# Engine loops over four tiles in two sorted expert mixtures, and who copies the weights

## The chip, the cores and the metric

The program runs on one core of a Trainium2 chip. The metric is the device time of one execution in microseconds. The core's engines are PE (TensorE: matrix products and transposes), DVE (VectorE), ACT (ScalarE), POOL (GpSimd) and SP (SyncE, which here only issues transfers). Each has its own instruction stream; they meet at semaphores.

## The reference, cut to what matters

A network of four layers on 128 graphs of 40 nodes with 128 features, 5120 tokens in all; each layer is a graph step and an expert mixture or another token step. Two of the mixtures are computed by sorted tiles in the kernel, layer 1's and layer 3's:

```python
def _L1_ffn_ref(x, gamma, beta, Wr, br, W1, b1, W2, b2):   # E = 8 experts, top 2, 128 -> 256 -> 128
    xn = (x - mu) * rsqrt(var + EPS) * gamma + beta
    logits = einsum('bsd,de->bse', xn, Wr) + br
    top_vals, top_idx = top_k(logits, 2)
    w = softmax(top_vals); w_full = ...                      # the gate of each token for each expert
    for e in range(E):
        h = gelu(einsum('bsd,dh->bsh', xn, W1[e]) + b1[e])
        y = y + (einsum('bsh,hd->bsd', h, W2[e]) + b2[e]) * w_full[..., e, None]

def _L3_ffn_ref(x, Wg, bg, W1, b1, W2, b2):                 # the same with 8 experts, top 2, gates of 1
    ...
```

Layer 2's token step is a graph attention over 524288 edges (plus one loop a node) that yields gate scores. For it the kernel must know, for each node, how many edges with a source beyond the tokens point at it. That count is independent of the mixture of layer 1, and the kernel does it beside that mixture:

```python
src = concatenate([edge_index[0], loops]); dst = concatenate([edge_index[1], loops])
e = leaky_relu(a_src[src] + a_dst[dst], 0.2)
ee = exp(e - segment_max(e, dst)[dst]); denom = segment_sum(ee, dst)
```

## The kernel before

`graph_network` calls the layers in order; each stage has one instruction stream for every engine, and a stage ends when all its engines are done. In the two sorted mixtures a router picks two experts for each token and gives each of the 10240 pairs of token and expert a place in a list that is sorted by expert and padded to tiles of 256 rows. `ex.NT` = 47 tiles is the most that this can need, and all 47 are always computed. `ex.table` holds the expert of each tile, `ex.gidx` the token of each place, `ex.pidx` the two places of each token.

`sparse_moe` is run twice: for layer 1 with `count` (an `EdgeCount`) and for layer 3 without it. A tile i goes through these steps.

- POOL gathers its 256 token rows from DRAM by two indirect transfers of 128 rows (L1126), into one of `NX` = 6 buffers. It may write tile i once PE has transposed tile i-6 (semaphore `x_ps`).
- PE transposes the rows (`turned`, L1148).
- ACT moves the transposed rows out of PSUM (`moved`, L1192, or L1194 with layer 1's scale and shift), and copies the expert's 642 columns of weights into one of `NW` = 3 buffers (`fetch`, L1209).
- PE does the hidden products (`hidden`, L1157), ACT the two gelus (`gelus`, L1202), PE the output products (`outer`, L1165).
- DVE adds the bias and writes the result (`result`, L1229), SP stores it to DRAM (L1281), from one of `NY` = 4 buffers.

The order on each engine is fixed by the Python loops, which write out all 47 tiles. PE's is: transposes of tile i+2, hidden products of i+1, output products of i. ACT's: gelus of i, move of i+2, copy of the weights of i+2.

Behind the tiles, when all stores have landed, POOL gathers the two result rows of every token (L1138): 8 parts of 5 token tiles, ten indirect transfers a part, 80 in all, into 6 buffers. DVE adds each part into the residual (L1268 with gates in layer 1, L1270 in layer 3), and in layer 3 SP stores the output.

The edge count of layer 1 works on `keys`, 4096 numbers in each partition. `find` (L1882) takes the eight largest of a segment, `strike` (L1887) puts zero in their place. Segments of 64 come first (64 of them), then segments of 256 (16); in the kernel before DVE does two finds and two strikes beside each tile, over tiles 0 to 41. Then `rest` (L1912 to L1916) tests how many keys are left and takes the largest number over the partitions, PE turns that column (`count_left`, L1952), and `size` makes from it the number of turns of a wide search. `digits` (L1891 to L1902) splits the 640 keys found into two digits, and then the keys are counted in 40 batches of 16: `one_hot` (L1908, L1909) writes two comparison tables, and `counts` (L1957) multiplies them in PE, 16 products into one accumulator. Two table buffers are used in turn, so DVE's batch c waits for PE's batch c-2 (`h_ps` of the count), and PE's batch c waits for DVE's (`hot`). In the kernel before all 40 batches come behind the tiles, five ahead of each of the eight parts' additions. `finish` (L1932 on) is last: a loop with a number of turns from the data, each with four finds and strikes over 1024 keys, the digits, and two batches; then the sums are copied out (L1944), and the next layer can begin.

```python
for n in range(PARTS):                       # DVE, behind the tiles
    if count is not None:
        step = count.KS // count.HG // PARTS
        for c in range(n * step, (n + 1) * step):
            count.one_hot(dve, c, c % 2, c * count.HG)
```

## Time and profile before

| what | us |
|---|---|
| median of 3 runs | 3664.99 |
| the runs | 3655.89 to 3667.97 |
| the profiled execution | 3670.82 |
| its span, first to last instruction | 3669.0 |
| DVE, PE, ACT, POOL busy in it | 2320.1, 2788.3, 1256.7, 584.0 |

The profile is of one execution. A row of a timeline gives the start from the beginning of the span, the duration, the engine, the line, the operation, what it writes and reads, and in brackets how long the engine was idle before it and what ended that, as far as the profile can tell. Rows of one line that follow each other closely are merged (x8). PE's ends are modelled, since its products are pipelined. The name of a releaser that is an input transfer of long ago ("DMA xin") stands for one the profile could not tell. PEclk is the granted clock as a share of full speed; DMA is the busy share of the 16 transfer engines.

### The profile page before, as it was taken

The page shows a single profiled execution, that of the slowest core. Times are in us where ns is not written, and L with a number is a line of the kernel's source. Part 1 is how long each engine was busy: PE and PEld are TensorE (multiplying, and loading weights), DVE is VectorE, ACT ScalarE, POOL GpSimd, SP SyncE. Part 2 cuts the span into 40 slices and gives each one's busy share as a digit, 9 for nine tenths or more (in the row PEclk, how much of TensorE's full clock was granted, in tenths as well). Part 3 has the DMA queues.
Part 4 walks back from the last instruction along what each step waited for, and adds up shares of the span by engine and source line. Part 5 has one row for each costly group of instructions (what it writes and reads, how often), then busy time and mean ns, then how long its engine had stood idle before and what let it go on. Part 6 is the DMA issues. An engine that isn't in the chain of part 4 may idle for free. (4 is left out here: it accounts for less than half of the span.)

```text
span 3669.0 us, 53910 instructions
## 1 busy us (share of the span) xinstructions
PE 2788.3 (76%) x20509; PEld 1774.0 (48%) x20509; DVE 2320.1 (63%) x4225; ACT 1256.7 (34%) x2409; POOL 584.0 (16%) x561
## 2 busy tenths in 40 slices
PE   6479999999999999463575249699876989985660
PEld 5234555555555555252264237366543666652550
DVE  6736777777777777468535395788993346765111
ACT  3333434444344444143262004222112444543440
POOL 0000000000000000100165400133220013420556
PEclk7689999999999999766597556799987987886785
DMA  3312111121111112112033110000001211102232
GB/s 40 99 39 51 41 39 39 45 56 39 41 52 39 39 39 50 60 35 58 14 87 61 33 16 1 5 0 0 1 0 47 66 41 46 44 16 58 70 80 72
DMA packets 163983, 151.93 MB, mean 41 GB/s; under 512 B 73412, under 2 KB 139344, under 8 KB 161320
## 3 DMA queue, kind: packets, MB, share of 16 engines
q1 hardware_dynamic: 152624, 126.06, 14.0%
q0 software_dynamic: 11136, 22.83, 3.0%
q8 instruction: 148, 2.42, 0.3%
q14 instruction: 75, 0.61, 0.1%
HBM read 123.16 MB, written 25.67 MB: 41 GB/s over the span
## 5 line engine op out<-in xcount | busy, mean ns | idle before, releaser
L2821 PE MATMUL hy_ps<-hy_uT,hy_win 128*128 128x512 f32 x1152 | 498.7, 594 | 0.0
L2821 PEld LDWEIGHTS hy_ps<-hy_uT,hy_win 128*128 128x128 f32 x1152 | 217.6, 190 | 281.2 <-issue 281.2
L2882 PE MATMUL hy_ps<-hy_wo,hy_yg 128*128 128x512 f32 x512 | 245.0, 624 | 10.1 <-ACT XNP L3018 8.6
L2347 PE MATMUL er_c<-XNG 128*128 128x400 f32 x544 | 205.1, 517 | 24.6 <-POOL XNG L2278 24.4
L1791 POOL IOTA iof<- 128x128 f32 x1 | 0.2, 243 | 1394.6 <-POOLq L2494 1394.6
L1126 POOL DMA_INDIRECT f_xg<-f_xn,f_gidx x188 | 178.2, 948 | 173.8 <-POOLq L893 76.7
L1229 DVE TENSOR_TENSOR f_ysl<-f_py,f_cur 128x256 f32<-128x256 f32 x94 | 38.4, 420 | 229.8 <-PE f_py L1165 124.0
L1957 PE MATMUL f_px<-XNG 128*128 128x40 bf16 x736 | 69.2, 266 | 143.3 <-DVE XNG L1909 98.0
L1138 POOL DMA_INDIRECT XNP<-f_y,f_pidx x160 | 160.3, 1002 | 85.0 <-issue 48.1
L2278 POOL TENSOR_TENSOR XNG<-er_VW,er_MD 128x400 f32<-128x400 f32 x136 | 122.3, 899 | 295.5 <-DVEq L2248 196.9
L2292 ACT ACTIVATE er_OT<-er_t 128x384 bf16<-128x384 f32 x128 | 61.0, 489 | 307.9 <-PE er_t L2317 307.9
L1157 PE MATMUL f_ph<-f_xT,f_cur 128*128 128x256 f32 x376 | 110.9, 422 | 60.4 <-issue 54.4
L2882 PEld LDWEIGHTS hy_ps<-hy_wo,hy_yg 128*128 128x128 f32 x512 | 96.0, 197 | 124.8 <-issue 102.9
L3095 DVE TENSOR_TENSOR_SCAN XNG<-XNG,hy_fx 128x2048 f32<-128x2048 f32 x32 | 141.6, 4425 | 2.3
L2347 PEld LDWEIGHTS er_c<-XNG 128*128 128x128 f32 x544 | 98.6, 193 | 85.2 <-POOL XNG L2278 27.8
L2327 PE MATMUL er_g<-er_TP,er_OT 128*128 128x320 bf16 x768 | 130.8, 308 | 10.1 <-ACT er_OT L2292 6.1
L1957 PEld LDWEIGHTS f_px<-XNG 128*128 128x128 bf16 x736 | 60.7, 152 | 151.8 <-DVE XNG L1909 106.0
L836 DVE TENSOR_TENSOR f_hg<-f_hs,f_gb 128x640 f32<-128x640 f32 x64 | 52.7, 825 | 110.1 <-ACT f_hs L818 110.1
L1165 PEld LDWEIGHTS f_py<-f_cur,f_hT 128*128 128x128 f32 x752 | 106.6, 207 | 20.2 <-issue 13.7
L1165 PE MATMUL f_py<-f_cur,f_hT 128*128 128x128 f32 x752 | 108.2, 291 | 10.6 <-issue 10.2
L2969 ACT ACTIVATE hy_xr<-hy_ps 128x512 f32<-128x512 f32 x80 | 47.5, 593 | 178.3 <-PE hy_ps L2821 178.3
L1562 PE MATMUL g_ps<-g_Z,g_wc 128*128 128x320 f32 x256 | 106.1, 562 | 1.1 <-ACT g_Z L1625 1.1
(652 smaller groups left out, 6310.2 us busy)
## 6 DMA issues: line engine op xcount, KB each, us to landing
XNG<-hy_decays SPq DMA_DIRECT2D x32, 1024.0 KB
hy_rb<-hy_inverse SPq DMA_DIRECT2D x128, 128.0 KB, 3.3
f_y<-f_ysl SPq DMA_DIRECT2D x94, 128.0 KB
f_gb<-gate_rows SPq DMA_DIRECT2D x16, 640.0 KB, 5.2
g_KB<-g_keys SPq DMA_DIRECT2D x32, 320.0 KB
f_xn<-XNG SPq DMA_DIRECT2D x4, 1280.0 KB
hy_xn<-XNP SPq DMA_DIRECT2D x1, 4096.0 KB, 14.1
hy_XC<-hy_xn SPq DMA_DIRECT2D x16, 256.0 KB
```

The source lines that it names most:

```text
L1126: pool.indirect_dma_start(out=xg[:, i % NX, h, :], out_offset=None, in_=ex.xn_dram, in_offset=bass.IndirectOffsetOnAxis(ap=ex.gidx[:, n:n ...
L1138: pool.indirect_dma_start(out=yc[:, n % NC_, t, c, :], out_offset=None, in_=ex.y_dram, in_offset=bass.IndirectOffsetOnAxis(ap=ex.pidx[:, n ...
L1157: pe.matmul(psh[i % 2][k], cur[:, i % NW, k * 128:(k + 1) * 128], xT[:, i % 2, :], start=True, stop=True).then_inc(h_ps, 1)
L1165: mm = pe.matmul(psy[i % 2][:, h, :], hT[:, i % 2, k, h * 128:(h + 1) * 128], cur[:, i % NW, H + k * D:H + (k + 1) * D], start=(k == 0), s ...
L1562: mm = pe.matmul(psy, wc[:, h, :], Z[:, c % 2, h].rearrange("p b n -> p (b n)"), start=(h == 0), stop=(h == HD - 1))
L1957: mm = pe.matmul(self.ph, self.OL[:, b, :, k], self.OH[:, b, :, k], start=False, stop=False, skip_group_check=True)
L2278: pool.tensor_tensor(X[:, u % XBUF], VW[:, 1 - par, u, :, None].broadcast_to([128, V, TJ]), MD[:, 1 - par, u, None, :].broadcast_to([128, ...
L2327: pe.matmul(o[:, 0:NS], OT[:, u % 2, j, :], TP[:, i, j * NS:(j + 1) * NS], start=(i == 0 and j == 0), stop=(i == 2 and j == J - 1))
L2347: mm = pe.matmul(flat(acc[j][:]), OD[:, 1 - par, u, j * 128:(j + 1) * 128], flat(X[:, u % XBUF]), start=False, stop=False, skip_group_chec ...
L2821: mm = pe.matmul(p[:], win[:, t, m * 128:(m + 1) * 128], uT[:, t, :], start=(t == 0), stop=(t == KT - 1))
L2882: mm = pe.matmul(PS[4 + q % 2][:], yg[:, t, q * 128:(q + 1) * 128], wo[:, t, :], start=(t == 0), stop=(t == KT - 1))
L3095: dve.tensor_tensor_scan(L[:, a][:, st], dAb[:, a][:, st], E[:, st], 0.0, ALU.mult, ALU.add)
```

## The change

Both mixtures compute 48 tiles, twelve turns of `BODY` = 4. PE, ACT, SP, and in the last mixture DVE, run the first and the last turn written out and those between as a loop of their own (`Fori`), with waits and addresses from a register. POOL stays written out. All three sorts of buffer become four (from 6, 4 and 3). The hidden products of a tile go to one PSUM bank instead of two, and signal once instead of twice. The count gets two banks of its own.

In the last mixture DVE copies the weights, three tiles ahead of its sums; in the first ACT does, as before.

The count of layer 1 is laid out anew. DVE does three finds and strikes of 64 beside each of the first 22 tiles, two of 256 beside each of the next 8, the test of what is left and the digits at tile 30 and the reduction at tile 31. Beside tiles 32 to 47 it writes one batch of tables each, and PE counts that batch behind the output products of the same tile. The wide search comes right behind the tiles, ahead of the parts; the 24 batches that remain come three ahead of each part's additions.

```diff
+BODY = 4
-        self.NT = (2 * T + E * (SL - 1)) // SL
+        self.NT = -(-((2 * T + E * (SL - 1)) // SL) // BODY) * BODY
...
-    NX, NY, NW = 6, 4, 3
+    NX, NY, NW = BODY, BODY, BODY
+    TURNS = NT // BODY
...
-        psh = [[bank(f"ph{i}{k}") for k in range(K)] for i in range(2)]
+        psh = [bank(f"ph{i}").rearrange("p (k n) -> p k n", k=K) for i in range(2)]
         if count is not None:
-            count.borrow(psx[0], psx[1])
+            count.borrow(bank("pc"), bank("pt"))
+            COUNTING = count.FIRST // BODY
...
         def _(pe):
...
                 for k in range(K):
-                    pe.matmul(psh[i % 2][k], cur[:, i % NW, k * 128:(k + 1) * 128], xT[:, i % 2, :], start=True, stop=True).then_inc(h_ps, 1)
+                    mm = pe.matmul(psh[j % 2][:, k, :], cur[:, j % NW, k * 128:(k + 1) * 128], xT[:, j % 2, :], start=True, stop=True)
+                mm.then_inc(h_ps, 1)
...
+            def tiles(r, final=False, counting=None):
+                for j in range(BODY):
+                    if not (final and j + 2 >= BODY):
+                        turned(r + (j + 2) // BODY, (j + 2) % BODY)
+                    if not (final and j + 1 >= BODY):
+                        hidden(r + (j + 1) // BODY, (j + 1) % BODY)
+                    outer(r, j)
+                    if counting is not None:
+                        count.counts(pe, BODY * counting + j, j % 2)
+            turned(0, 0)
+            turned(0, 1)
+            hidden(0, 0)
+            tiles(0)
+            if count is None:
+                with pe.Fori(1, TURNS - 1) as r:
+                    tiles(r)
+                tiles(TURNS - 1, final=True)
+            else:
                 count.count_start(pe)
+                with pe.Fori(1, COUNTING) as r:
+                    tiles(r)
+                with pe.Fori(0, TURNS - 1 - COUNTING) as r:
+                    tiles(r + COUNTING, counting=r)
+                tiles(TURNS - 1, final=True, counting=TURNS - 1 - COUNTING)
                 count.count_left(pe)
-                for c in range(count.KS // count.HG):
-                    count.counts(pe, c, c % 2)
                 count.count_rest(pe)
...
         def _(act):
...
+            def tiles(r, final=False):
+                for j in range(BODY):
+                    gelus(r, j)
+                    if not (final and j + 2 >= BODY):
+                        moved(r + (j + 2) // BODY, (j + 2) % BODY)
+                        if count is not None:
+                            fetch(r + (j + 2) // BODY, (j + 2) % BODY)
...
         def _(dve):
...
+            def fetch(r, j):
+                i = BODY * r + j
+                e = dve.value_load(ex.table[0:1, bass.ds(i, 1)], min_val=0, max_val=E - 1)
+                if not (isinstance(i, int) and i < NW):
+                    dve.wait_ge(y_out, i - NW + 1)
+                dve.tensor_copy(cur[:, j % NW, :], ex.W[:, bass.ds(e, 1), :].rearrange("p a n -> p (a n)")).then_inc(w_cur, 1)
...
+                with dve.Fori(1, TURNS - 1) as r:
+                    for j in range(BODY):
+                        result(r, j)
+                        fetch(r + (j + 3) // BODY, (j + 3) % BODY)
...
+                for i in range(NT):
+                    result(i // BODY, i % BODY)
+                    count.beside_tile(dve, i)
                 count.size(dve)
+                count.wide(dve)
             for n in range(PARTS):
                 if count is not None:
+                    count.beside_part(dve, n, PARTS)
...
+    FIRST, EARLY = 32, 16
...
+    def beside_tile(self, dve, i):
+        fine, mid = EC // self.FINE, EC // self.MID
+        fine_tiles, mid_tiles = -(-fine // 3), mid // 2
+        f = lambda t: min(3 * t, fine)
+        if 1 <= i <= fine_tiles:
+            dve.drain()
+            self.strike(dve, self.FINE, 0, f(i - 1), f(i))
+        if i < fine_tiles:
+            self.find(dve, self.FINE, 0, f(i), f(i + 1))
+        m = i - fine_tiles
+        if 0 <= m <= mid_tiles:
+            dve.drain()
+            if m > 0:
+                self.strike(dve, self.MID, self.KF, 2 * m - 2, 2 * m)
+            if m < mid_tiles:
+                self.find(dve, self.MID, self.KF, 2 * m, 2 * m + 2)
+        if m == mid_tiles:
+            dve.drain()
+            dve.tensor_scalar(self.left, self.keys, 0.0, None, ALU.is_gt)
+            self.digits(dve, slice(0, self.KS))
+        if i == self.FIRST - 1:
+            dve.tensor_reduce(self.seg[:], self.left.rearrange("p (s c) -> p s c", c=WIDE), AX.X, ALU.add)
+            dve.drain()
+            dve.tensor_reduce(self.cnt[:], self.seg[:], AX.X, ALU.max).then_inc(self.counted, 1)
+        if i >= self.FIRST:
+            c = i - self.FIRST
+            self.one_hot(dve, c, c % 2, c * self.HG)
...
-                self.one_hot(dve, KS // HG + r * (KW // HG) + c, c % 2, KS + c * HG)
-        dve.wait_ge(self.h_ps, n * (KW // HG) + KS // HG + 3)
+                self.one_hot(dve, self.EARLY + r * (KW // HG) + c, c % 2, KS + c * HG)
+    def beside_part(self, dve, n, parts):
+        late = self.KS // self.HG - self.EARLY
+        for c in range(n * late // parts, (n + 1) * late // parts):
+            self.one_hot(dve, self.EARLY + self.turns * (self.KW // self.HG) + c, c % 2, (self.EARLY + c) * self.HG)
+    def close(self, dve):
+        dve.wait_ge(self.h_ps, self.turns * (self.KW // self.HG) + self.KS // self.HG + 3)
         dve.tensor_copy(self.g.cntB[:], self.ph)
...
+        late = KS // HG - self.EARLY
+        with pe.Fori(0, late // 2) as r:
+            for c in range(2):
+                self.counts(pe, self.EARLY + n * (KW // HG) + 2 * r + c, c)
```

## Rows read from the trace of the kernel before

**Rows 1.** the page: the span and the chain that ended last, by engine.
```profile
span 3669.0 us, 53910 instructions
...
PE 3%; POOL 2%; issue 1%; another core or an unknown queue 1%; DMA 0%; ACT 0%; DVE 0%; POOLq 0%; ACTq 0%; DVEq 0%
```

**Rows 2.** windows; busy of PE, PEld, DVE, ACT, POOL; PEclk, DMA share, GB/s.
```profile
1811.00:1930.00 119.00, 78.75 (x472) 68.79 (x472) 36.34 (x219) 67.66 (x137) 76.83 (x81) 0.88 0.30 79
...
1966.00:2081.00 115.00, 19.90 (x209) 17.23 (x209) 37.18 (x60) 0.00 (x0) 81.71 (x80) 0.52 0.19 47
2081.00:2186.00 105.00, 49.67 (x529) 43.65 (x529) 100.07 (x184) 0.00 (x0) 0.00 (x0) 0.50 0.00 1
3403.00:3556.00 153.00, 112.57 (x658) 98.25 (x658) 18.74 (x47) 87.08 (x189) 88.72 (x94) 0.86 0.36 80
```

**Rows 3.** timeline of POOL in the first mixture: start us, us, instruction, idle before.
```profile
1875.80 0.94 POOL L1126 DMA_INDIRECT f_xg<-f_xn,f_gidx  x1 [1.26 <-PE f_px L1148]
...
1881.78 0.94 POOL L1126 DMA_INDIRECT f_xg<-f_xn,f_gidx  x1 [1.28 <-PE f_px L1148]
```

**Rows 4.** timeline of PE, same stretch.
```profile
1871.10 1.10 PE L1157 MATMUL f_ph<-f_xT,f_cur 128*128 128x256 f32 x4 [1.79 <-issue]
1872.04 1.05 PE L1165 MATMUL f_py<-f_cur,f_hT 128*128 128x128 f32 x8
```

**Rows 5.** timeline of DVE, same stretch.
```profile
1875.53 0.42 DVE L1229 TENSOR_TENSOR f_ysl<-f_py,f_cur 128x256 f32<-128x256 f32 x1 [3.54 <-PE f_py L1165]
```

**Rows 6.** timeline of DVE at the end of the last mixture's tiles.
```profile
3550.04 0.42 DVE L1229 TENSOR_TENSOR f_ysl<-f_py,f_cur 128x256 f32<-128x256 f32 x1 [1.55 <-PE f_py L1165]
...
3554.67 0.42 DVE L1229 TENSOR_TENSOR f_ysl<-f_py,f_cur 128x256 f32<-128x256 f32 x1 [0.47 <-PE f_py L1165]
```

**Rows 7.** timeline of all engines behind the first mixture's last tile.
```profile
1965.07 0.42 DVE L1229 TENSOR_TENSOR f_ysl<-f_py,f_cur 128x256 f32<-128x256 f32 x1 [0.47 <-PE f_py L1165]
...
1968.14 0.94 POOL L1138 DMA_INDIRECT XNP<-f_y,f_pidx  x1 [18.64 <-DMA f_y<-f_ysl]
...
2029.30 1.53 PE L1957 MATMUL f_px<-XNG 128*128 128x40 bf16 x16 [7.71 <-DVE XNG L1909]
...
2055.65 1.23 DVE L1908 TENSOR_TENSOR XNG<-XNG,ec_dl 128x2048 bf16<-128x2048 bf16 x1 [26.41 <-DMA xin<-in_x_dram]
...
2056.79 0.48 DVE L1909 TENSOR_TENSOR XNG<-XNG,ec_dh 128x640 bf16<-128x640 bf16 x1
...
2072.99 0.94 POOL L1138 DMA_INDIRECT XNP<-f_y,f_pidx  x1 [0.30 <-issue]
2080.89 1.23 DVE L1908 TENSOR_TENSOR XNG<-XNG,ec_dl 128x2048 bf16<-128x2048 bf16 x1 [23.61 <-DMA xin<-in_x_dram]
...
2083.97 2.87 DVE L1268 SCALAR_TENSOR_TENSOR raw<-XNP,f_gates,raw 128x128 f32<-128x128 f32 x10
```

**Rows 8.** timeline of DVE in the wide search and at the layer's end.
```profile
2140.66 4.60 DVE L1882 MAX8 ec_K<-lend 128x8 f32<-128x1024 f32 x4
...
2155.07 4.60 DVE L1882 MAX8 ec_K<-lend 128x8 f32<-128x1024 f32 x4
...
2185.61 0.20 DVE L1944 COPY cntB<-f_px 128x40 f32<-128x40 f32 x1 [1.64 <-PE f_px L1967]
```

**Rows 9.** DVE groups, 1811 to 2187, by form: busy us, mean ns, idle before.
```profile
L1882 DVE MAX8 ec_K<-lend 128x8 f32<-128x64 f32 x64 | 11.0, 214 | 0.0
...
L1914 DVE TENSOR_REDUCE ec_seg<-XNG 128x4 f32<-128x4096 f32 x1 | 4.4, 4420 | 0.1
L1912 DVE TENSOR_SCALAR XNG<-lend 128x4096 f32<-128x4096 f32 x1 | 2.3, 2294 | 0.1
```

**Rows 10.** window of the stage that loops on registers; columns as in rows 2.
```profile
2820.00:2960.00 140.00, 140.00 (x500) 92.11 (x499) 54.62 (x74) 61.10 (x117) 0.00 (x0) 1.00 0.25 66
```

**Rows 11.** windows of DVE's sums (L1229) alone; columns as in rows 2, DVE alone.
```profile
1811.00:1930.00 119.00, 13.40 (x32) 0.88 0.30 79
```

**Rows 12.** POOL's gathers behind both mixtures (L1138): count, min/median/max ns.
```profile
L1138 POOL DMA_INDIRECT XNP<-f_y,f_pidx x160: 940/944/1679, 1968.1 to 3659.4; - x160
```

More of the change, by code:

```diff
@@ L1127, in gather @@
                                             in_offset=bass.IndirectOffsetOnAxis(ap=ex.gidx[:, n:n + 1], axis=0)).then_inc(x_in[i % NX], 16)
[L1129 to L1130 removed]
             for b in range(NY):
[L1132 removed]
+                pool.wait_ge(y_st[b], 16 * TURNS)
             for n in range(PARTS):
@@ L1203, in gelus @@
                 ins.then_inc(h_out, 1)
-            def fetch(i):
-                e = act.value_load(ex.table[0:1, i:i + 1], min_val=0, max_val=E - 1)
-                if i >= NW:
-                    act.wait_ge(y_out, i - NW + 1)
-                act.activation(cur[:, i % NW, :], ex.W[:, bass.ds(e, 1), :].rearrange("p a n -> p (a n)"), ACT.Copy).then_inc(w_cur, 1)
-            act.wait_ge(ex.w_in, 16 * (2 * K + 2))
-            for i in range(NW):
-                fetch(i)
-            moved(0)
@@ L1215, in _ @@
-            moved(1)
-            for i in range(NT):
-                gelus(i)
-                if i + 2 < NT:
-                    moved(i + 2)
-                if i >= 1 and i - 1 + NW < NT:
-                    fetch(i - 1 + NW)
+            def tiles(r, final=False):
[5 more added lines that the diff above has]
+                            fetch(r + (j + 2) // BODY, (j + 2) % BODY)
@@ L1223, in _ @@
+            act.wait_ge(ex.w_in, 16 * (2 * K + 2))
+            if count is not None:
+                fetch(0, 0)
+                fetch(0, 1)
+            moved(0, 0)
+            moved(0, 1)
+            tiles(0)
+            with act.Fori(1, TURNS - 1) as r:
+                tiles(r)
+            tiles(TURNS - 1, final=True)
         @block.vector
         def _(dve):
-            def result(i):
-                dve.wait_ge(y_ps, i + 1)
-                if i >= NY:
-                    dve.wait_ge(y_st[i % NY], 16 * (i // NY))
-                dve.tensor_tensor(y[:, i % NY], psy[i % 2], cur[:, i % NW, None, 2 * H:2 * H + D].broadcast_to([128, SLH, D]), ALU.add).then_inc(y_out, 1)
@@ new lines, in _ @@
+            if count is None:
+                dve.wait_ge(ex.w_in, 16 * (2 * K + 2))
+                for j in range(3):
+                    fetch(0, j)
+                for j in range(BODY):
+                    result(0, j)
+                    fetch((j + 3) // BODY, (j + 3) % BODY)
+                with dve.Fori(1, TURNS - 1) as r:
+                    for j in range(BODY):
+                        result(r, j)
+                        fetch(r + (j + 3) // BODY, (j + 3) % BODY)
+                for j in range(BODY):
+                    result(TURNS - 1, j)
+                    if j + 3 < BODY:
+                        fetch(TURNS - 1, j + 3)
+            else:
@@ L1274, in _, with store @@
             if count is not None:
-                count.finish(dve)
+                count.close(dve)
         @block.sync
         def _(sp):
-            for i in range(NT):
+            def store(r, j):
+                i = BODY * r + j
                 sp.wait_ge(y_out, i + 1)
-                sp.dma_start(ex.y_dram[i * SL:(i + 1) * SL, :].rearrange("(h p) d -> p h d", p=128), y[:, i % NY]).then_inc(y_st[i % NY], 16)
+                sp.dma_start(ex.y_dram[bass.ds(i * SL, SL), :].rearrange("(h p) d -> p h d", p=128), y[:, j]).then_inc(y_st[j], 16)
+            with sp.Fori(0, TURNS) as r:
+                for j in range(BODY):
+                    store(r, j)
             if out is not None:
```

120 lines of the change are left out of this document (44 added, 76 removed).

## The prediction

> **What bounds the kernel now.** I read the page first: one core, 3669.0 us of span, and a chain of waits that ends with POOL's gathers in the last mixture and says nothing of the first, so the two mixtures have to be read stage by stage [rows 1]. The windows by stage come next [rows 2]. In both mixtures no engine is full: in the first one's tiles PE is busy 78.75 of 119 us and POOL 76.83; in the stage after it (1966 to 2081) DVE is busy 37 of 115 us, and only from 2081 to 2186 is something full, DVE with 100.07 of 105 us. So I look for waits.
>
> In the tile loop the reader should lay three timelines side by side [rows 3 to 5]. POOL issues four gathers 1.25 us apart (0.94 and 0.3 of issue), then waits 1.28 us for PE's transposes. PE has a tile's output products under way from 1872.04 to 1873.09. DVE, which needs nothing but their end, idles 3.54 us and starts the sum at 1875.53, 2.4 us after it; the next tile's sum follows at once, and the next pair comes as POOL's pairs do, 5.98 us on. Two tiles cost four gathers (5.0 us) plus about 0.97 us: 2.98 us a tile. Where no gathers are left, a sum is 0.42 us after 1.55 us of idle: 1.98 us a tile [rows 6]. So PE's signals arrive late while POOL issues gathers, and the loop's rate is the gathers' plus what is let through between them. What makes them late no view shows.
>
> The stage after the first mixture shows the same thing undiluted [rows 7]. POOL issues 80 gathers back to back to 2073.93. PE counts a batch from 2029.30 and is done in 1.53 us; DVE's batch at 2055.65 waits for PE's counts and comes after 26.41 us of idle, the next at 2080.89 after 23.61 us, and from 7 us past POOL's last gather everything runs at DVE's own speed. Of 40 early batches and 8 additions 13 and 2 are done by 2080. The rest, with three turns of the wide search (14.4 us each [rows 8]), is the full DVE of the window 2081 to 2186 [rows 2], and the next layer waits for its end at 2185.81 [rows 8].
>
> **The change, part by part.** Times are of the profiled execution (3670.82 us, span 3669.0); the median of the runs is 3664.99, 5.8 us less, and I carry the difference over.
>
> One tile more in each mixture (48 for 47): the first has it inside the term for tiles 32 to 47, the second pays 2.97 us, at least 1.98 [rows 3, 6].
>
> Loops. A stage that already loops on register waits has PE busy for 140.00 of 140.00 us [rows 10]. Register waits and branches cost nothing there, and I take 0. The bound above is one of PE's present "issue" waits, 1.79 us [rows 4], at each branch back: ten turns a mixture, of which the gathers cover all but the four on the ring below, 7 us. Below zero, fewer instructions to load might end those waits altogether; that is rival A. The Trainium skill speaks against the loops: "Runtime: NRT & Kernel Launch", section "Instruction fetch mechanics", says that a taken branch to code outside the pages held stalls the engine for a fetch, and prefers unrolled code; by it the bound above would be in the sum. Rows 10 show no such stall in a loop with a smaller body; for a body this long no run here shows it yet.
>
> Tiles 0 to 31 of the first mixture. The gathers set the rate, and they stay. DVE does three finds and strikes a tile for two: a find is 0.214 us [rows 9], its strike by my estimate 0.3, beside a tile of 2.98 us, so 0. At tiles 30 and 31 it gets the test of what is left (2.29), seven digit operations (estimated at 3.6 together) and the reduction (4.42 us) [rows 9]: some 10 us of DVE over two tiles, of which two tiles of lead hide about 6, so +4. With four gather buffers for six POOL has issued two tiles less when result 31 is out, 2 x 2.5 = -5 us. Sum 0 (-5 to +5): sum 31 stays just before 1930, as the 32 in that window show [rows 11].
>
> Tiles 32 to 47. Here PE gets a batch of 16 counting products behind each tile's output product, and that batch needs the one-hots which DVE writes after the *same* tile's sum. What was parallel becomes a ring: output product, sum 0.42, one-hots 1.14 + 0.48, signal 0.07, counts 1.53, then the next tile's transposes, hidden and output products 1.98 and 0.25 until its end is seen: 5.87 us [rows 6, 7]. Of these the signal (DVE's second one-hot row to PE's start), the two parts of the products (0.22 a pair of transposes, 0.86 and 0.9) and the 0.25 are read off the starts of PE's rows. The two gathers that the transposes set free run 2.5 us beside the 1.98 us of products, so the late signal adds between 0 and the 1.3 us that POOL itself waits now [rows 3]; I take 0.55, thus 6.4 us a tile, 102 us for 16. Below, with the counts at half their time at the higher clock (1.53 us was at a granted 0.50 to 0.52, [rows 2]): 5.1 us a tile, 82. Above, all of the 1.3 us: 7.2, 115. Before, the 15 tiles left at 1930 took until 1965.1 [rows 7]. The tiles' end moves from there to 1929 + 102 = 2031.
>
> The tail. POOL: 3.07 us until the last store has landed, then 80 gathers, to T+109 (T the last sum; before 1965.07 to 2073.93) [rows 7]. Everything runs free at T+116. Meanwhile DVE has the three wide turns, 43 us, and then 24 batches (40 less 16) in 8 parts. Before, five batches passed between T+47 and T+116; I take five again and one part's additions of 2.87 us. Left at T+116: 19 x 1.62 + 7 x 2.87 = 51 us, end at T+167. Bound below: nothing held, T+119. Above: the wide turns held as well, nothing else done, T+116 + 39 + 23 = T+178. Before it was T+220.7, so this edit gives back 54 us (43 to 102).
>
> First mixture: 2031 + 167 = 2198 for 2185.8, +12 us: the ring costs 66 us, the tail returns 54.
>
> Second mixture. Its copies of the weights go from ACT to DVE, which is busy 18.74 of 153 us [rows 2]. ACT is busy 87 of 153 us and holds up no gather, so its relief is worth 0; with one 0.4 us copy a tile DVE has time. Three things remain: the tile more, +3; four buffers for six, which leave less banked for the end at 1.98 us a tile, -5 to 0, taken at -3; and the copies' effect on POOL. Some gathers of the tail take up to 1.68 us for 0.94 [rows 12]; the long ones lie beside DVE's one-hots. DVE's copy of 642 elements, by the 4096-element operation of 2.294 us, is 0.36 to 0.42 us [rows 9], and could lengthen a gather by 0 to 0.42 us, 0 to 20 us over 48 tiles; I take 3, since mostly it falls in POOL's own wait. Sum +3 (-6 to +20). The Trainium skill, "SBUF — State Buffer", section "SBUF: two separate sides", says that a float32 copy within SBUF on DVE locks GpSimd out of writing descriptors until it ends; by it the copies would count in full wherever they meet a gather, which is rival C.
>
> Total: +12 +3 = +15 us, 3665 + 15 = 3680 us.
>
> **Rivals.** *A, the hold goes.* If PE's late signals come from the long unrolled stream and not from POOL, the loops end them: tiles at the gathers' 2.5 us, the ring at 5.87, the tail at T+119. First mixture 1930 - 32 x 0.48 + 94 + 119 = 2128, -58; second 47 x 0.48 = -23, and +3: -78 us, 3587. For it: PE's idle is put down to "issue" [rows 4]. Against: the last tiles are unrolled too and run at 1.98 us [rows 6]. 8%.
>
> *B, the tail flows.* DVE's work lengthens some of POOL's gathers [rows 12], and signals pass more often there than later, when DVE stands still; in the changed tail DVE has the wide search to do. It decides from about a dozen batches that get through beside the gathers. With 15 batches and 5 additions, 9 x 1.62 + 3 x 2.87 = 23 us are left, the end at T+139, and with nothing added to the ring (5.87, 94 us) 1929 + 94 + 139 = 2162, -24; with the second mixture's +3: 3644. Against: the last three batches of before took 60 us. 20%.
>
> *C, slower by far: DVE shuts POOL out.* Its place is each gather of the second mixture that a copy meets, and in the ring each that a one-hot meets; it decides once most are met. The copies then cost 20 us for 3, the ring 7.2 us a tile for 6.4 (+13): +45 us, 3710. For it rows 12; against, the copies start just where POOL waits. 16%.
>
> **How the numbers follow.** My forecast, ring (66 us) against tail (54 us), has 56%; the bounds of its terms, not all at one end, make its own range -15 to +40 us, 3650 to 3705. A has 8%, B 20%, C 16%. The range for 8 in 10 leaves out A and the outer parts of B and C: 3634 to 3712. A measurement here can tell 0.3%, 11 us. Faster by more: A and B, 28%. Within: the lower part of the forecast, 24%. Slower: the rest of it, 32%, with C 16%: 48%.
>
> **What would show it.** In the changed trace: sums of tiles 32 to 47 6.4 us apart, with DVE's one-hots between and PE waiting for them; tiles before that near 2.98 us and gathers 1.25 us apart with waits of about 1 us; the wide search (1024-wide finds) beside POOL's 80 gathers, none behind them; some 19 batches after the last gather, and the layer's end 167 us after the last sum. In the second mixture the last sum within 10 us of where it was (3554.67 in the span, [rows 6], moved by what the first mixture gives), and gathers with a mean of 0.94 to 1.1 us. Wrong would be: sums 32 to 47 under 5 us apart, or any tile stage near 2.5 us (A), batches passing freely beside POOL (B), gathers of 1.3 us and more in the second mixture (C).

## The result, and the profile after

The changed kernel takes 3671.25 us in the median of 20 runs (3658.61 to 3695.19), the kernel before 3660.68 us in 20 runs of the same study (3614.33 to 3678.17). The ratio is 1.0053, interval 1.0032 to 1.0074: slower, by about 11 us, where 15 us were forecast. The profiled execution has a span of 3673.6 us.

The page says as little of the mixtures as the one before: the span, and a chain that again lies in the last mixture.

```profile
span 3673.6 us, 54903 instructions
...
PE 2%; POOL 2%; issue 1%; ACT 0%; another core or an unknown queue 0%; DMA 0%; DVE 0%; ACTq 0%; POOLq 0%; SPq 0%; DVEq 0%
```

The windows by stage, with the columns of [rows 2]. The stages are cut at the first gather (1823), sum 31 (1941), the last sum (2050), POOL's sixtieth gather of the tail (2130) and the copied counts (2207).

```profile
1823.00:1941.00 118.00, 82.26 (x471) 71.05 (x471) 54.39 (x281) 69.29 (x139) 76.20 (x78) 0.86 0.29 78
1941.00:2050.00 109.00, 72.72 (x442) 64.41 (x442) 34.77 (x50) 28.57 (x54) 16.96 (x18) 0.69 0.15 31
2050.00:2130.00 80.00, 6.23 (x65) 5.33 (x65) 28.58 (x50) 0.00 (x0) 57.55 (x60) 0.50 0.20 51
2130.00:2207.00 77.00, 40.53 (x433) 35.62 (x433) 74.55 (x154) 0.00 (x0) 26.18 (x20) 0.50 0.07 17
3407.00:3559.00 152.00, 113.13 (x672) 98.34 (x672) 44.56 (x96) 56.93 (x145) 93.02 (x96) 0.90 0.36 81
```

Set beside [rows 2]: tiles 0 to 31 take 118 us as before. Tiles 32 to 47, which took 36 us as 15 tiles, take 109; PE is busy 72.72 us of it, and no other engine is near full. The granted clock of 0.69 there is a mean of the two levels, which change places within each tile. The tail falls in two halves: 80 us in which DVE is busy 28.58 (waiting again), and 77 us in which it is busy 74.55. The second mixture's tiles take 152 us with DVE at 44.56 for 18.74 and ACT at 56.93 for 87.08.

The stage lengths, each read off its first and last row in the trace (us):

| stage | before | after | forecast of the difference |
|---|---|---|---|
| sum 31 to the last sum, first mixture | 35.9 | 108.4 | +66 |
| last sum to the counts copied | 220.7 | 157.0 | -54 |
| first gather to the counts copied | 374.7 | 383.0 | +12 |
| last mixture, first gather to last sum | 151.6 | 151.9 | +3 |
| last sum to the end of the span | 114.4 | 114.8 | 0 |

In the two profiled executions the stages outside the mixtures differ too: the first gather came 12.2 us later and the stretch from the first mixture to the last was 16.7 us shorter. The second is mostly one group of products in layer 3's graph step, the same instructions at another mean duration, first before, then after:

```profile
L1562 PE MATMUL g_ps<-g_Z,g_wc 128*128 128x320 f32 x256 | 106.1, 562 | 1.1 <-ACT g_Z L1625 1.1
```

```profile
L1593 PE MATMUL g_ps<-g_Z,g_wc 128*128 128x320 f32 x256 | 94.1, 509 | 1.1 <-ACT g_Z L1656 1.1
```

It is not the change's: a later profile of the kernel before (e11) has these 256 products at 511 ns, and one of a kernel with the change (e9) at 548. What makes them shorter in one execution than in another was not tried.

One period of the ring in tiles 32 to 47 (start, us, instruction, idle time before), after the last of POOL's gathers:

```profile
2009.96 0.42 DVE L1253 TENSOR_TENSOR f_ysl<-f_py,f_cur 128x256 f32<-128x256 f32 x1 [4.91 <-issue]
2010.31 1.21 DVE L1940 TENSOR_TENSOR XNG<-XNG,ec_dl 128x2048 bf16<-128x2048 bf16 x1
2011.44 0.48 DVE L1941 TENSOR_TENSOR XNG<-XNG 128x640 bf16<-128x640 bf16 x1
...
2011.98 1.50 PE L2015 MATMUL f_pc<-XNG 128*128 128x40 bf16 x16 [2.05 <-DVE XNG L1941]
...
2013.30 0.64 PE L1147 MATMUL f_px<-ident,f_xg 128*128 128x128 f32 x2
...
2013.73 1.91 PE L1157 MATMUL f_ph<-f_xT,f_cur 128*128 128x256 f32 x4
...
2015.44 1.33 PE L1167 MATMUL f_py<-f_cur,f_hT 128*128 128x128 f32 x8
...
2016.81 0.42 DVE L1253 TENSOR_TENSOR f_ysl<-f_py,f_cur 128x256 f32<-128x256 f32 x1 [4.89 <-PE f_py L1167]
```

The sum of one tile is at 2009.96, that of the next at 2016.81. DVE's one-hots follow the sum at once, PE idles 2.05 us for them, counts for 1.32 us, then transposes (0.43), does the hidden products (1.71) and the output products, whose end DVE sees 1.37 us after their start. That is the ring as forecast, in its order; but the products of a tile took 3.5 us from transposes to sum where I had taken 1.98 and 0.25.

The granted clock says why (windows of PE alone: its busy time, PEclk, DMA share, GB/s; a batch of counts and the output products near the start of the ring, then the idle time, the hidden and the output products of the period above):

```profile
1947.89:1949.22 1.33, 1.33 (x17) 0.50 0.01 1
1951.35:1953.27 1.92, 1.92 (x9) 0.50 0.24 64
2009.96:2011.98 2.02, 0.00 (x1) 1.00 0.60 62
2013.73:2015.44 1.71, 1.71 (x6) 0.50 0.00 0
2015.44:2016.79 1.35, 1.33 (x9) 0.79 0.00 0
```

In this period the clock stands at the upper level while PE is idle and falls to the lower one (0.50) while it works. The four hidden products take 1.71 us at it, the eight output products 1.92 at 0.50 and 1.35 at 0.79.

The tail:

```profile
2068.16 3.06 PE L2015 MATMUL f_pc<-XNG 128*128 128x40 bf16 x32 [15.05 <-DVE XNG L1941]
...
2086.16 1.23 DVE L1940 TENSOR_TENSOR XNG<-XNG,ec_dl 128x2048 bf16<-128x2048 bf16 x1 [5.25 <-DMA xin<-in_x_dram]
...
2127.19 0.94 POOL L1136 DMA_INDIRECT XNP<-f_y,f_pidx  x1 [0.30 <-issue]
2129.56 1.23 DVE L1940 TENSOR_TENSOR XNG<-XNG,ec_dl 128x2048 bf16<-128x2048 bf16 x1 [41.77 <-DMA xin<-in_x_dram]
...
2153.58 3.62 POOL L1136 DMA_INDIRECT XNP<-f_y,f_pidx  x1 [25.44 <-DVE raw L1294]
...
2206.15 0.19 DVE L2002 COPY cntB<-f_pc 128x40 f32<-128x40 f32 x1
```

PE counts two batches by 2071.2. DVE's next one-hot, which needs the first of them, comes at 2086.16, and the one that needs the second at 2129.56, after 41.77 us of idle. It is 1.4 us after POOL's sixtieth gather ended: POOL then stood still by itself, since it fills six part buffers and DVE had emptied none (25.44 us of idle until 2153.58). From 2129.56 on DVE runs at its own speed.

### The profile page after: what moved, and what is told of

Its sections match the earlier page's. It is cut to its first block and busy times, and to the rows that moved or that the text cites. A ratio compares the mean times of both kernels' runs of the same rounds, so it can differ in the third digit from the quotient of the medians.

```text
span 3673.6 us, 54903 instructions
## 1 busy us (share of the span) xinstructions
PE 2812.4 (77%) x20537; PEld 1792.5 (49%) x20537; DVE 2344.9 (64%) x4276; ACT 1233.2 (34%) x2370; POOL 594.1 (16%) x565
## 5 line engine op out<-in xcount | busy, mean ns | idle before, releaser
L1127 POOL DMA_INDIRECT f_xg<-f_xn,f_gidx x192 | 186.3, 970 | 217.9 <-PE f_px L1147 80.1
L2015 PE MATMUL f_pc<-XNG 128*128 128x40 bf16 x736 | 69.1, 266 | 147.1 <-DVE XNG L1941 130.1
L1157 PE MATMUL f_ph<-f_xT,f_cur 128*128 128x256 f32 x384 | 124.3, 455 | 43.2 <-issue 27.8
L2015 PEld LDWEIGHTS f_pc<-XNG 128*128 128x128 bf16 x736 | 60.6, 152 | 156.3 <-DVE XNG L1941 139.3
L1167 PEld LDWEIGHTS f_py<-f_cur,f_hT 128*128 128x128 f32 x768 | 117.5, 221 | 26.9 <-ACT f_hT L1225 14.4
L1167 PE MATMUL f_py<-f_cur,f_hT 128*128 128x128 f32 x768 | 118.7, 305 | 14.2 <-ACT f_hT L1225 12.4
L1157 PEld LDWEIGHTS f_ph<-f_xT,f_cur 128*128 128x128 f32 x384 | 79.0, 228 | 58.7 <-issue 38.4
## 6 DMA issues: line engine op xcount, KB each, us to landing
hy_rb<-hy_inverse SPq DMA_DIRECT2D x128, 128.0 KB, 3.3
f_y<-f_ysl SPq DMA_DIRECT2D x96, 128.0 KB
```

Of the source, the lines that this page charges most:

```text
L1127: pool.indirect_dma_start(out=xg[:, i % NX, h, :], out_offset=None, in_=ex.xn_dram, in_offset=bass.IndirectOffsetOnAxis(ap=ex.gidx[:, n:n ...
L1157: mm = pe.matmul(psh[j % 2][:, k, :], cur[:, j % NW, k * 128:(k + 1) * 128], xT[:, j % 2, :], start=True, stop=True)
L1167: mm = pe.matmul(psy[j % 2][:, h, :], hT[:, j % 2, k, h * 128:(h + 1) * 128], cur[:, j % NW, H + k * D:H + (k + 1) * D], start=(k == 0), s ...
L2015: mm = pe.matmul(self.ph, self.OL[:, b, :, k], self.OH[:, b, :, k], start=False, stop=False, skip_group_check=True)
```

## The experiments

Four kernels ran on one chip, four on a second and four on a third. What makes PE's signals late in [rows 3 to 7], the hold, was there on the first and third chip and not on the second, so the table says which. "Tiles" is sum 31 to the last sum of the first mixture, "tail" from there to the copied counts, "last" the last mixture from its first gather to its last sum, all in us.

| kernel | signals late | ratio to before, interval | tiles | tail | last |
|---|---|---|---|---|---|
| before, first profile | yes | | 35.9 | 220.7 | 151.6 |
| before, again (e11) | yes | 3630.79 us, one run | 36.1 | 191.0 | 151.3 |
| after, first profile | yes | 1.0053 (1.0032 to 1.0074) | 108.4 | 157.0 | 151.9 |
| after, again (e10) | yes | 1.0044 (1.0016 to 1.0072) | 106.1 | 164.9 | 154.8 |
| e1, counts one tile behind | yes | 0.9894 (0.987 to 0.9918) | 53.6 | 157.9 | 153.7 |
| e2, all batches behind the tiles | yes | 0.9924 (0.9896 to 0.9952) | 40.8 | 175.3 | 152.4 |
| e3, gaps in POOL's tail | yes | 1.0109 (1.0083 to 1.0135) | 108.0 | 184.0 | 152.7 |
| e4, more work on PE | yes | 1.0093 (1.0064 to 1.0122) | 108.4 | 179.2 | 152.1 |
| e9, e1 and ACT's copies | yes | 0.9863 (0.9796 to 0.993) | 53.2 | 158.8 | 154.8 |
| e12, e1 and a drain after ten | yes | 0.9857 (0.9789 to 0.9925) | 53.8 | 143.4 | 156.0 |
| e5, the same kernel as e12 | no | 0.9985 (0.9968 to 1.0002) | 53.8 | 143.5 | 135.0 |
| e6, e1 and a drain after five | no | 1.0054 (1.0035 to 1.0072) | 53.8 | 163.3 | 134.7 |
| e7, before and a drain after five | no | 1.0147 (1.0103 to 1.0191) | 41.3 | 212.7 | 128.0 |
| e8, after with ACT's copies | no | 1.0068 (1.0043 to 1.0092) | 107.3 | 120.8 | 132.2 |

**e1: is it the ring?**

```diff
-                    if counting is not None:
-                        count.counts(pe, BODY * counting + j, j % 2)
+                    if counting is not None and not (isinstance(counting, int) and counting == 0 and j == 0):
+                        count.counts(pe, BODY * counting + j - 1, (j - 1) % 2)
...
+                count.counts(pe, count.EARLY - 1, (count.EARLY - 1) % 2)
```

> The changed kernel, but in tiles 32 to 47 PE counts the batch of the tile before (batch c-1 behind the output product of tile 32+c, the sixteenth behind the last tile), so that no batch needs the one-hots written after the same tile's sum. Theory (the ring of output product, sum, one-hots, counts is what makes these tiles cost 6.8 us): the stretch from sum 31 to the last sum falls from 108 us to 16 tiles of 3 to 4 us, 48 to 64; the tail behind it stays at about 157 us; the whole is 45 to 55 us shorter, 0.985 to 0.99 of before. Rival (the stretch is slow because PE's signals are held and its clock is low, whatever the order): it stays above 95 us and the whole within 10 us of the changed kernel.

The stretch fell from 108.4 to 53.6 us with the same 16 batches in it, and the kernel is 1.1% faster than before instead of 0.5% slower. PE and DVE now work beside each other (timeline of e1):

```profile
1961.19 1.03 PE L1157 MATMUL f_ph<-f_xT,f_cur 128*128 128x256 f32 x4
...
1962.06 1.05 PE L1167 MATMUL f_py<-f_cur,f_hT 128*128 128x128 f32 x8
...
1962.95 1.47 PE L2017 MATMUL f_pc<-XNG 128*128 128x40 bf16 x16
...
1963.15 0.42 DVE L1255 TENSOR_TENSOR f_ysl<-f_py,f_cur 128x256 f32<-128x256 f32 x1 [1.32 <-PE f_py L1167]
1963.49 1.22 DVE L1942 TENSOR_TENSOR XNG<-XNG,ec_dl 128x2048 bf16<-128x2048 bf16 x1
...
1964.62 0.48 DVE L1943 TENSOR_TENSOR XNG<-XNG 128x640 bf16<-128x640 bf16 x1
...
1966.43 0.43 DVE L1255 TENSOR_TENSOR f_ysl<-f_py,f_cur 128x256 f32<-128x256 f32 x1 [1.32 <-PE f_py L1167]
```

```profile
1929.00:1983.00 54.00, 48.66 (x435) 46.66 (x433) 34.53 (x49) 26.44 (x53) 16.58 (x17) 0.91 0.43 61
```

Sums are 3.28 us apart, PE has no idle time in these rows, and the hidden products take 0.87 us from their start to the output products' (1.71 in the ring). So moving the order alone also gave the products their speed back; the windows from sum 31 to the last sum have a granted clock of 0.91 for 0.69. The counts gained nothing by the clock (window of PE in e1, one batch):

```profile
1962.95:1964.24 1.29, 1.29 (x19) 1.00 1.21 51
```

That is 1.29 us at 1.00, for 1.33 at 0.50 in the ring. The theory holds: the ring was worth 54.8 us. The rest over the 40.8 us of e2, 12.8 us, is what 16 batches cost beside the tiles without a ring.

**e2: the two halves of the count's change apart.**

```diff
-    FIRST, EARLY = 32, 16
+    FIRST, EARLY = 32, 0
...
-        if i >= self.FIRST:
-            c = i - self.FIRST
-            self.one_hot(dve, c, c % 2, c * self.HG)
```

> The changed kernel with no batch beside the tiles: all 40 batches come behind them, five ahead of each part, still behind the wide search. Theory (ring costs 66 to 72 us, moving 16 batches off the tail and the wide search forward gives the rest back): tiles end 36 us after sum 31 as before (108 in the changed kernel); the tail is 116 us of gathers, then 35 batches of 1.62 and 7 parts' additions of 2.87, some 190 us (157 in the changed kernel, 220 before); the whole 30 to 40 us shorter than the changed kernel, 0.99 to 0.995 of before. Rival (what shortened the tail is the moved batches alone, the wide search's place being worth nothing): the tail is 210 us or more, the whole within 0.3% of before.

With all 40 batches behind the tiles and the wide search ahead of them the tail is 175.3 us, for 220.7 (in a second profile 191.0) in the kernel before; with 16 batches gone from it, 157.0. So the wide search's new place gave 45 us by the first profile of before (16 by the second), the moved batches 18, and e2 is 0.76% faster than before. The medians lie between the two profiles: e2 is 27.7 us faster with tiles that take 4.9 us longer, which leaves some 33 us for the tail if the rest is equal (an estimate). Both expectations of e2 overstated the tail. One long wait is left here too (timeline of DVE in e2):

```profile
2011.99 1.24 DVE L1938 TENSOR_TENSOR XNG<-XNG,ec_dl 128x2048 bf16<-128x2048 bf16 x1 [4.48 <-issue]
...
2054.69 1.25 DVE L1938 TENSOR_TENSOR XNG<-XNG,ec_dl 128x2048 bf16<-128x2048 bf16 x1 [29.98 <-issue]
```

**e3 and e4: what holds DVE in the tail?**

```diff
+                        if count is not None and (2 * t + c) % 5 == 4:
+                            for _ in range(2):
+                                pool.drain()
+                                pool.memset(xg[:], 0.0)
```

> The changed kernel, but in the first mixture's tail POOL fills a spent buffer twice (about 2 us) after every fifth of the 80 gathers. Theory (PE's signals to DVE stand still while POOL issues gathers back to back, and pass when it pauses): DVE's waits of 42 us in the tail shrink to the length of five gathers, 7 us or less; POOL needs 137 us for the tail instead of 106 plus waits, the layer's end comes 142 to 152 us after the last sum (157 now). Rival (the waits have another cause, PE's or DVE's own): waits over 15 us remain, and the end moves out to 170 us or more.

```diff
                 self.counts(pe, self.EARLY + r * (KW // HG) + c, c % 2)
+                for _ in range(8):
+                    pe.matmul(self.more, self.zero[:], self.zero[:], start=True, stop=True)
```

> The changed kernel, but behind each counting batch of the tail PE issues eight more products of zeros into an unused part of a bank, about 1 us, with no signal. Rival to the theory above (a batch's signal leaves PE only when more work follows it there, and PE is idle in the tail): DVE's waits of 5 and 42 us fall under 2 us, and the end comes 120 to 130 us after the last sum. Theory (POOL's gathers hold it): the waits stay over 20 us in sum, the end stays at 150 to 165 us.

In e3 no wait of DVE for PE over 3 us is left in the tail. What DVE waits for is the gathers themselves, a part every 22 us:

```profile
2126.28 2.02 POOL L1141 MEMSET f_xg<- 128x1024 f32 x2 [1.83 <-issue]
...
2136.08 2.88 DVE L1298 SCALAR_TENSOR_TENSOR raw<-XNP,f_gates,raw 128x128 f32<-128x128 f32 x10 [14.56 <-DMA XNP<-f_y,f_pidx]
...
2158.58 2.88 DVE L1298 SCALAR_TENSOR_TENSOR raw<-XNP,f_gates,raw 128x128 f32<-128x128 f32 x10 [14.86 <-DMA XNP<-f_y,f_pidx]
```

The pause was 4 us and not 2 (the drain alone holds POOL 1.8 us behind its last gather, then come two fills of 0.95 us and a second drain; the first pause was 11 us), and there are 16: POOL's tail went from 133 to 176 us and set the end. The mechanism is as the theory had it, the forecast of the time was wrong by the size of the pause.

In e4 the end came 22 us later, not earlier (179.2 us, outside the 150 to 165 of the theory too, which had not counted the time of the added products): more work on PE pushes no signal out. Its trace shows more than that (timeline of PE and DVE in e4):

```profile
2072.02 0.27 PE L2027 MATMUL f_pt<-ec_zero 128*128 128x128 bf16 x1 [2.53 <-issue]
...
2074.83 0.26 PE L2027 MATMUL f_pt<-ec_zero 128*128 128x128 bf16 x1 [2.54 <-issue]
...
2118.59 0.95 POOL L1136 DMA_INDIRECT XNP<-f_y,f_pidx  x1 [0.30 <-issue]
...
2125.22 0.27 PE L2027 MATMUL f_pt<-ec_zero 128*128 128x128 bf16 x1 [1.13 <-issue]
...
2125.92 0.27 PE L2027 MATMUL f_pt<-ec_zero 128*128 128x128 bf16 x1 [0.43 <-issue]
...
2128.06 1.23 DVE L1941 TENSOR_TENSOR XNG<-XNG,ec_dl 128x2048 bf16<-128x2048 bf16 x1 [50.19 <-DMA xin<-in_x_dram]
```

These zero products and the batch behind them wait for nothing that the profile shows, and PE starts one every 2.1 or 2.8 us for as long as POOL gathers (forty had gone at full speed before, from 2059.55 to 2063); some 6 us after POOL's last gather before its stop they come 0.70 us apart, and then at full speed. So not only PE's signals are late: PE itself gets on by about one product in two gathers. Whether both are one thing, and where in the chip it sits, these runs don't show.

**e5 to e8: on a chip without the hold.** The edit of e5 and e6 is e1's and a `pool.drain()` after every tenth (fifth) gather of the first tail; e7 is the kernel before with a drain after every fifth; e8 lets ACT copy the weights of the last mixture, two tiles ahead, and takes the copies from DVE. Drain and e8:

```diff
+                        if count is not None and (2 * t + c) % 10 == 9:
+                            pool.drain()
...
                         moved(r + (j + 2) // BODY, (j + 2) % BODY)
-                        if count is not None:
-                            fetch(r + (j + 2) // BODY, (j + 2) % BODY)
+                        fetch(r + (j + 2) // BODY, (j + 2) % BODY)
...
                     for j in range(BODY):
                         result(r, j)
-                        fetch(r + (j + 3) // BODY, (j + 3) % BODY)
```

> The kernel with PE's counts one tile behind, and in the first mixture's tail a drain of POOL after every tenth of the 80 gathers. In the run with gaps a drain ended 1.9 us after the last gather. Theory (PE is held by POOL's unbroken gathers and let go in any pause): eight pauses of 2 us let two or three batches through each; DVE's wait of 42 us becomes several of at most 12 us, the tail 135 to 150 us (158 without the drains), the whole 8 to 23 us less than 3614. Rival (a pause of 2 us after ten gathers is too short to clear what has piled up): the tail stays at 155 to 175 us.

> The same with a drain after every fifth gather. Theory: no wait of DVE for PE over 8 us; POOL itself needs 80 x 1.25 + 16 x 2 = 132 us and ends the tail at 135 to 145 us after the last sum. Rival: waits over 15 us remain and the tail is 165 us or more.

> The kernel before, with nothing of the change, and a drain of POOL after every fifth gather of the first mixture's tail. Theory (the hold of PE's signals was what DVE waited for there, and so what the wide search's new place and the moved batches give back): the batches flow beside the gathers, which end 135 us after the last sum; the wide search of 43 us follows; the tail is 175 to 190 us for 220.7, the whole 30 to 45 us faster than before (0.988 to 0.992). Rival (pauses too short, or the hold another thing): the tail stays within 10 us of 220, or grows to 245 with POOL's pauses.

> The changed kernel, but in the last mixture ScalarE copies the weights, two tiles ahead, as in the first. Theory (DVE's copies lengthen some of POOL's gathers by little, and ScalarE's load holds nothing up): from the first gather to the last sum 149 to 152 us for 152 to 154 in the runs with DVE's copies, and gathers of 0.944 us in the mean again. Rival (DVE's copies save time, by taking work out of the chain from transposes to hidden products): 155 us or more.

On this chip the kernel before took 3567.09 us (3663.5 and 3656.7 on the two others), and e8, which has the changed first mixture unaltered, shows why (timeline of DVE and PE in its tail):

```profile
2035.31 3.04 PE L2007 MATMUL f_pc<-XNG 128*128 128x40 bf16 x32 [15.05 <-DVE XNG L1933]
...
2047.50 0.94 POOL L1136 DMA_INDIRECT XNP<-f_y,f_pidx  x1 [0.30 <-issue]
...
2048.21 1.23 DVE L1932 TENSOR_TENSOR XNG<-XNG,ec_dl 128x2048 bf16<-128x2048 bf16 x1 [0.15 <-issue]
2048.75 1.50 POOL L1136 DMA_INDIRECT XNP<-f_y,f_pidx  x1 [0.30 <-issue]
```

With POOL's gathers 1.25 us apart, DVE's one-hot at 2048.21 needs the batch of 2035.31 and waits for nothing. The tail is 120.8 us; the 119 of my lower bound was worked out for just this. Tiles come 2.65 us apart in the first 31 for 3.3. The ring is as long as with the hold, 107.3 us. The drains cost time here and bring nothing: e5's tail is 22.7 us longer than e8's. e5 to e7 therefore don't test their theory, which was about a hold that wasn't there, and the tails of e6 and e7 missed their ranges (163.3 for 135 to 145, 212.7 for 175 to 190): sixteen drains cost more than the 2 us each that were taken for them, POOL's gathers took 155 us in e6 for 132. e7 (1.0147) shows only the price of 16 pauses. And e8, the changed kernel but for the copies, is 21 us (0.68%) slower than before here. Ten of these show beside e7, whose tiles are those of the kernel before: 82.0 us for 76.2 in tiles 0 to 31, and 132.2 for 128.0 in the last mixture. So there the change has costs that the hold hides. The rest is the ring against what the tail gives back; the kernel before has no profile on this chip, so how much less its tail had to give is argued and not shown.

e8 does tell of the copies: the last mixture's tiles take 132.2 us with ACT's and 134.7 and 135.0 with DVE's, and the mean of its 96 gathers is 0.944 us for 0.974 and 0.979: DVE's copies cost 2.5 to 2.8 us without the hold (one profile of each kernel; their gathers differ by about 3 us in sum, 90.6 us in e8, 94.0 and 93.5 in e5 and e6). With the hold the difference is lost in the spread (154.8 in e9 and in e10).

**e9 to e12: both kernels and the two best versions on one chip**, which has the hold.

> The changed kernel with both its costs taken out: PE counts the batch of the tile before, and ScalarE copies the weights in the last mixture too. Theory (the ring costs 54 us, DVE's copies 2 to 3 us): 55 to 60 us less than the changed kernel of the same call, whether PE's signals are held in this run or not; where they are held 0.985 to 0.99 of before, where not 0.987 to 0.995. Rival (DVE's copies cost nothing and the ring's share depends on the hold): within 50 us of the changed kernel.

> The changed kernel itself, for its stages beside those of the kernel before in the same call. Theory (ring plus 67, wide search's place minus 45 where PE's signals are held in the tail, moved batches minus 18): where they are held, as in the first profiles, the first mixture 6 to 10 us longer than before and the whole 1.003 to 1.007; where they are not held (gathers 1.25 us apart without a pause in the tiles, no DVE wait over 10 us in the tail), the tail is 121 us and there is less to give back: 20 to 30 us slower, 1.005 to 1.008 of before. Rival (the two kernels differ by the same amount whatever holds): first mixture plus 8 in both.

> The kernel before itself, for its profile in this call. Theory: with the hold the tail from the last sum to the copied counts is 220 us and the tiles 3.3 us apart in the mean of the first 31; without it DVE does its batches beside the gathers and the tail is about 109 + 45 to 55 us, 155 to 165, tiles 2.5 us apart. Rival (the hold is the kernel's own, not the run's): 220 us in any run.

> Counts one tile behind, and a drain of POOL after every tenth gather of the first tail. Theory: where PE's signals are held, the tail is 140 to 150 us for 158 without the drains and the whole 8 to 18 us faster than with the lag alone; where they are not held the drains cost 23 us, as 143.5 us of tail against 120.8 showed. Rival: with the hold the tail stays over 155 us.

The ratio of the changed kernel repeats (1.0044), but not the 6 to 10 us expected of its first mixture: that takes 390.9 us, 16 more than in the first profile of before and 44 more than in e11. e9, with the counts one tile behind and ACT's copies, is 65 us below it in the medians (3614.51 and 3679.72), 55 to 60 were expected. The drain after ten gathers now does what it was made for: the tail is 143.4 us for 158.8, and DVE waits for gathers alone (timeline of DVE in e12):

```profile
2118.75 2.88 DVE L1298 SCALAR_TENSOR_TENSOR raw<-XNP,f_gates,raw 128x128 f32<-128x128 f32 x10 [8.29 <-DMA XNP<-f_y,f_pidx]
...
2134.80 2.88 DVE L1298 SCALAR_TENSOR_TENSOR raw<-XNP,f_gates,raw 128x128 f32<-128x128 f32 x10 [8.36 <-DMA XNP<-f_y,f_pidx]
```

In the whole e12 and e9 can't be told apart: 3613.99 and 3614.51 us, with intervals of 0.7% on either side. So the 8 to 18 us that the drains were to give over the lag alone show in the tail of one profile and not in the medians; e1 itself did not run on this chip. Both beat both kernels. Since e12's drains cost 23 us on a chip without the hold, e9 is the version to take; it was not run on such a chip.

The second profile of the kernel before shows that its tail has no fixed length: 191.0 us, where 220 or 155 to 165 were expected. DVE's waits are the same in kind but shorter, each about the length of two to three gathers (timeline of DVE in e11):

```profile
2046.59 1.22 DVE L1908 TENSOR_TENSOR XNG<-XNG,ec_dl 128x2048 bf16<-128x2048 bf16 x1 [4.12 <-DMA xin<-in_x_dram]
...
2050.92 1.23 DVE L1908 TENSOR_TENSOR XNG<-XNG,ec_dl 128x2048 bf16<-128x2048 bf16 x1 [2.71 <-PE f_px L1957]
```

That execution took 3630.79 us, 33 us less than the median of its chip, and its tail is 30 us shorter than in the first profile, which was 6 us over its median. So some 30 us of swing lie in this tail, the loss by the change swings with it, and 220 us is nearer to the usual length than 191.

## Why the prediction came out right, point by point

*Where the waits are.* Right: both profiles after show them in the places named, and e3, e8 and e12 show that they go when POOL pauses or when the hold is absent.

*Ring.* Forecast 6.4 us a tile and 102 us to the last sum, measured 6.78 and 108.4. The order of the ring and its start at tile 32 were right, and e1 shows that the ring and not the batches costs most of it. The terms of the sum were not: 6.4 was 5.87 for the ring and 0.55 for late signals. The period shown above, 6.85 us, is 2.02 from the sum to the counts (2.11 taken), 1.32 of counts (1.53) and 3.5 of products to the sum (2.23). The mis-sized term is the last, taken from [rows 6] at the upper clock. I had put the two levels of the clock on the counts alone, and it is the other way round: a batch of counts takes 1.33 us at 0.50 and 1.29 at 1.00, the hidden products 1.71 and 0.87. Nor did the late signals add the 0.55. The first tiles of the ring are 7.43 us apart and the later ones 6.84, but e8, without the hold, goes from 7.43 to 6.83 as well, and at 7.43 the output products take 1.92 us at the lower clock for 1.35 later. A term too small by 1.3 us and three too large by 0.85 together leave the 0.4 us a tile that the forecast was off.

*Tail.* Forecast T+167, measured T+157.0, by another sum. I had five batches and a part pass beside the gathers, and freedom at T+116, when POOL's last gather is done. In fact no late batch passed, as in my upper bound, and the third wide turn stuck as well; but DVE was free at T+80.2, because POOL has six buffers for eight parts and stopped there. From then a wide turn of 14.4, 24 batches of 1.62 and 8 parts of 2.87 make 76 us, the end at T+156. The step that failed is "80 gathers, to T+109": the last one ended at T+136.2. I had read the buffers and not asked who empties them when DVE stands still. The two errors nearly cancel.

*Second mixture.* Forecast +3, measured +0.7 with its rest. The tile more and the lost head start are hidden in the hold; without it the last mixture takes 132.2 us in e8 for 128.0 in e7, and the copies' 2.5 us come on top. The bounds of -6 and +20 were added wrongly; the three terms give -3 and +23.

*Loops, tiles 0 to 31.* Forecast 0: 103.5 and 103.1 us from sum 0 to sum 31. The 2.98 us a tile that I read off one pair of tiles is too short for either: 103.5 us are 3.34 a tile in the kernel before itself. The Trainium skill's warning of a stall at a taken branch to code outside the pages held ("Runtime: NRT & Kernel Launch", section "Instruction fetch mechanics") does not show in these tiles, seven turns of a loop on PE; whether the jump back leaves the pages held no view shows, and the hold could hide a short stall. Without the hold the same stretch is 76.2 us in e7 and 82.0 in e8; six gather buffers for four, other finds and the loops all lie in these 5.8 us, and they were not taken apart.

*The total.* That +15 us was forecast and 11 measured is in part luck. The ring cost 72.5 us for 66 and the tail gave back 63.7 for 54, two errors of opposite sign, and the tail of before alone swings by more than the whole difference.

*Rivals.* A, that the hold goes with the loops: fell, the waits are there in loops too. B, that the tail flows: it did on one chip, because the hold was absent there and not because of the change, and e8 was still slower than the kernel before. C, DVE's copies shut POOL out: right in kind and far too large in price (2.5 us for 20). The copies themselves are longer than my 0.36 to 0.42 us (group of DVE, last mixture, after):

```profile
L1260 DVE COPY f_cur<-f_W 128x642 f32 x48 | 25.7, 535 | 21.7 <-issue 11.7 <-DVE f_ysl L1253 8.3 <-PEq L894 1.6
```

By "SBUF — State Buffer", section "SBUF: two separate sides" of the Trainium skill a float32 copy of DVE keeps GpSimd from writing a gather's descriptors until the copy ends. In e5 and e6 the copies (24.9 and 24.8 us) cost the mixture 2.8 and 2.5 us; if the rule holds, about a tenth of them was met, which no view here shows directly.

## What to carry to other kernels

Work put "beside" a loop costs nothing only if no engine needs in the same turn what another has just made there; let the consumer lag by one turn. Price the products of a ring in which PE idles at the lower clock, as these were granted it until e1 took the idle time away, but only those that a trace shows to follow the clock: the hidden and output products did, the counts did not. Where an engine waits for a slow signal, ask which buffer stops the engine that causes the delay: that, and not its last instruction, may be when the waiting ends. And give a stage's length from more than one profile before a gain is booked against it.

## What the runs showed of the hardware that was not expected

While POOL issues indirect gathers 1.25 us apart, PE's signals to DVE came up to 58 us late (a batch counted by 2071.2, its waiter at 2129.56), and in e4 PE started products that wait for nothing only every 2.1 to 2.8 us. Pauses of POOL of 2.7 us after ten gathers (e12) or 4 us after five (e3), the first of each tail 9 to 11 us, ended that. On one of three chips it did not occur at all, with the same instructions and the same gathers; that chip ran the kernel before in 3567 us for 3657 and 3663. Each chip was measured once, so whether the chip makes the difference or its condition at the time is not shown. A single gather took 3.62 us for 0.94 where DVE's one-hots lay beside it (the row at 2153.58); its cause was not tried.

The granted clock did not touch all products alike. A batch of 16 counting products (40 columns each) took 1.33 us at 0.50 and 1.29 at 1.00; four hidden products (256 columns) took 1.71 at 0.50 and 0.87 in e1 at 1.00.
